# Layer 2 of a two-layer transformer kernel from one table of steps, and three weight tiles loaded earlier

## The reference

```python
x = ln(x + softmax_attention(x))          # layer 1: 16 heads of 8, rope
x = ln(x + moe16(x))                      # 16 SwiGLU experts, grouped top 4, and a shared one
# layer 2
q, k, v = x @ Wq + bq, x @ Wk + bk, x @ Wv + bv
qf, kf = elu(q @ R) + 1, elu(k @ R) + 1   # 32 features a head
kv, ks = sum_s kf * v, sum_s kf
x = ln(x + (qf @ kv / max(qf @ ks, 1e-6)) @ Wo + bo)
g = top2(softmax(x @ Rt)); g = g / (sum(g) + 1e-6)     # 8 gates a token
x = ln(x + x @ W + b + (g * (x @ A)) @ B)
```

## Time and profile before

| | us |
|---|---|
| median of three runs | 527.77 |
| lowest and highest | 526.52, 531.72 |
| profiled execution, its own time | 527.63 |
| its span in the trace | 525.8 |
| TensorE busy | 481.0, 91% of the span |
| VectorE busy | 386.0, 73% |
| ScalarE, GpSimd busy | 224.6, 106.5 |
| mean granted TensorE clock | 0.952 of full speed |

### The profile page before, as it was taken

The page is one execution under the profiler, slowest core; times in us unless marked ns, Lnnn a source line. Parts: engine busy times, 40 slices in busy tenths (PEclk is TensorE's granted clock), DMA queues, the critical chain, the costliest instruction groups (busy, mean ns, idle before and its releaser), DMA issues. The chain is left out here.

```text
span 525.8 us, 7943 instructions
## 1 busy us (share of the span) xinstructions
PE 481.0 (91%) x2903; PEld 232.8 (44%) x2903; DVE 386.0 (73%) x994; ACT 224.6 (43%) x302; POOL 106.5 (20%) x101
## 2 busy tenths in 40 slices
PE   8889899999999999989979979999999999988772
PEld 3333233334333343333335545556557456545471
DVE  6398888887898888798629796974678466655553
ACT  2306657667766656656841222231332232233110
POOL 9880427006440010000100002000011001212020
PEclk9999999999999999999999999998999799879756
DMA  4854342224322333200132113112111000000000
GB/s 155 259 142 156 90 123 92 91 70 112 115 91 70 93 86 113 66 1 22 23 80 82 60 42 100 42 60 60 41 42 51 30 20 1 21 1 0 22 20 20
DMA packets 24878, 36.31 MB, mean 69 GB/s; under 512 B 2684, under 2 KB 16258, under 8 KB 24834
## 3 DMA queue, kind: packets, MB, share of 16 engines
q1 hardware_dynamic: 24840, 35.81, 23.3%
HBM read 24.07 MB, written 11.53 MB: 68 GB/s over the span
## 5 line engine op out<-in xcount | busy, mean ns | idle before, releaser
L1092 DVE TENSOR_REDUCE negmax<-psum 128x1 f32<-128x512 f32 x256 | 169.6, 687 | 34.0 <-PE psum L521 33.8
L805 ACT ACTIVATE probs<-psum 128x1024 f32<-128x1024 f32 x128 | 127.7, 1022 | 60.1 <-PE psum L537 57.7
L521 PE MATMUL psum<-KS,QS 125*128 125x512 bf16 x256 | 98.5, 385 | 7.4 <-DVE negmax L1092 4.1
L556 PE MATMUL psum<-probs,VA 128*32 128x256 f32 x1024 | 80.5, 390 | 0.4 <-ACT probs L805 0.4
L537 PE MATMUL psum<-QS,KS 128*128 128x512 bf16 x256 | 76.0, 380 | 0.1
L784 PE MATMUL psum<-xT,late 128*128 128x512 f32 x144 | 73.3, 634 | 0.0
L521 PEld LDWEIGHTS psum<-KS,QS 125*128 125x128 bf16 x256 | 24.5, 96 | 82.0 <-DVE negmax L1092 39.9
L448 POOL TENSOR_SCALAR var<-mv 128x4 f32<-128x4 f32 x16 | 4.3, 270 | 262.6 <-DVE mv L992 262.5
L915 ACT ACTIVATE QS<-psum 128x512 f32<-128x512 f32 x36 | 21.5, 597 | 65.2 <-PE psum L784 65.2
L771 PE MATMUL psum<-late,QS 128*128 128x128 f32 x288 | 40.6, 285 | 5.7 <-DVE QS L956 3.0
L1254 DVE SCALAR_TENSOR_TENSOR QS<-QS,psum 128x512 f32<-128x512 f32 x36 | 24.5, 680 | 26.1 <-ACT QS L915 26.1
(11 more groups left out here) (148 smaller groups left out, 590.0 us busy)
## 6 DMA issues: line engine op xcount, KB each, us to landing
stack_dram<-parts SPq DMA_DIRECT2D x24, 384.0 KB, 3.3
cw<-w_dram SPq DMA_DIRECT2D x32, 256.0 KB, 3.3
KS<-stack_dram SPq DMA_DIRECT2D x16, 288.0 KB
QS<-stack_dram SPq DMA_DIRECT2D x16, 288.0 KB
late<-in_late SPq DMA_DIRECT2D x8, 346.5 KB, 4.4
res<-in_x SPq DMA_DIRECT2D x4, 256.0 KB, 3.3
w_dram<-wT SPq DMA_DIRECT2D x4, 256.0 KB, 4.4
out_y<-KS SPq DMA_DIRECT2D x4, 256.0 KB, 2.2
```

What stands on the lines that cost most here:

```text
L521: mm(sm_bank(u)[:, :], QS[b % 2][0:KROW, h, qt * P:(qt + 1) * P], KS[b % 2][0:KROW, h, :], start=True, stop=True).then_inc(sm_full, 1)
L556: last_ = mm(ps[6][32 * j:32 * j + 32, q], VA[b % 2][:, kt, h, :], probs[:, n % 2, j, q], start=(kt == 0 and half == 0), stop=(kt == NT - ...
L805: fn(probs[:, n % 2, 2 * hf:2 * hf + 2, :], psum[:, 2 * hf:2 * hf + 2, :], ACT.Exp, scale=float(DH) ** -0.5).then_inc(exp_done, 1)
L1092: V.tensor_reduce(out=negmax[:, G % 4, i:i + 1], in_=sm_bank(u)[:, :], axis=X, op=ALU.max, negate=True).then_inc(sm_free, 1)
```

## The change

One table `steps` holds every step of layer 2 for one batch with its distance in pairs from pair 9(n+1). The loop places the table for each batch, newer batch first, so that of the steps that meet in one pair those of the newer batch come first. What falls behind pair 35 is `layer2`, in the order of that table, with no pairs between. `AT` to `norm3` of the last two batches come further apart from each other in that order, or in another order than before. Only steps beside pairs are `crowded` now. And SP issues the loads of the first three `cw` tiles right after the store of batch 0's weights, before it waits for those of batch 1.

```diff
-        beside = [[] for _ in range(NB * PAIRS + 12)]
+        beside = [[] for _ in range(NB * PAIRS + 25)]
...
-        a_round = (("K", 0, 0), ("AT", 1, 0), ("K", 0, 1), ("Y1", 1, 0), ("K", 0, 2), ("ghT", 2, 0), ("K", 0, 3),
-                   ("V", 0, 0), ("norm2", 1, 0), ("Y2", 2, 0), ("Q", 0, 0), ("Q", 0, 1), ("x3T", 1, 0), ("Q", 0, 2),
-                   ("norm3", 2, 0), ("lg", 1, 0), ("Q", 0, 3), ("KV", 0, 0), ("O", 0, 1), ("O", 0, 0), ("OT", 0, 1),
-                   ("OT", 0, 0))
-        round_at = (4, 4, 5, 5, 5, 6, 6, 7, 7, 7, 8, 8, 9, 9, 9, 10, 10, 11, 12, 12, 12, 12)
-        for n in range(NB):
-            w = PAIRS * (n + 1)
-            for at, kind in ((0, "chunk"), (1, "norm1"), (3, "x2T")):
-                beside[w + at].append((kind, n, 0))
-            if n + 1 < NB:
-                for (kind, back, c), at in zip(a_round, round_at):
-                    if n >= back:
-                        beside[w + at].append((kind, n - back, c))
+        steps = ((0, "chunk", 0), (1, "norm1", 0), (4, "x2T", 0), (5, "K", 0), (5, "K", 1), (6, "K", 2), (6, "K", 3),
+                 (7, "V", 0), (7, "Q", 0), (8, "Q", 1), (8, "Q", 2), (9, "Q", 3), (9, "KV", 0),
+                 (10, "O", 1), (10, "O", 0), (11, "OT", 1), (11, "OT", 0), (12, "AT", 0), (14, "Y1", 0), (15, "norm2", 0),
+                 (17, "x3T", 0), (18, "lg", 0), (21, "ghT", 0), (22, "Y2", 0), (23, "norm3", 0))
+        for n in reversed(range(NB)):
+            for at, kind, c in steps:
+                beside[PAIRS * (n + 1) + at].append((kind, n, c))
         layer2 = [s for one in beside[NB * PAIRS:] for s in one]
         del beside[NB * PAIRS:]
-        crowded = {s for one in beside for s in one} | set(layer2)
-        for n in range(last, NB + 2):
-            layer2 += [(kind, n - back, c) for kind, back, c in a_round if 0 <= n - back < NB]
+        crowded = {s for one in beside for s in one}
...
                     if kind == "combine":
                         store_weights(a)
-            for j in range(NB * EP):
+                        if a == 0:
+                            for j in range(CW):
+                                load_weights(j)
+            for j in range(CW, NB * EP):
```

## The result

The changed kernel took 536.59 us (median of 4 runs, 532.85 to 537.10) against 527.14 us of the kernel before, also a median of 4: 1.7% slower, ratio 1.017 with a 95% interval of 1.012 to 1.022. Its profiled execution has a span of 534.5 us (before: 525.8), 8.7 us more; I had summed 2.8. Lines of the changed kernel are numbered 6 lower from TensorE's part on (L784 is L778, L700 is L694).

A forecast was written before the change was run, and what follows sets the result against it. TensorE, busy 91% of the span, was taken as the bound, so time could come only from its pauses, low-clock work or their placement. Terms -2.7 -0.3 -2.8 +0.6 +4.3 -1.8 +6.5 -1.0 = +2.8 gave 530.4 us, range 523 to 536.

The forecast's parts named there:

- slower by over 1%: Outcome above 533.1 us, given 27%: the clock rival's 22%, half of the third and a little of the main case.
- Early loads: Pair 0: issuing the first `cw` loads sooner removes TensorE's wait before `down`, -2.7 us, bounds 0 and -3.3.
- The first `x2T`: Moved from pair 12 to 13 behind `down`: its 1.21 us wait goes, a quarter counted, -0.3 us.
- `OT` in a pair of its own: Beside the pairs, `x2T` of batch 2 loses its 1.24 us wait and the low clock behind it, -2.8 us.
- `ghT` of batch 1 ahead of `x2T`: Behind the pairs, late gates delay `x2T` and the first K of batch 3, +4.3 us, bounds +2.5 and +6.
- `x3T` of batch 2: Behind the pairs, `norm2` now precedes V, so its 1.76 us wait goes, -1.8 us.
- `ghT` and `Y2` of batch 2 ahead of `Y1`: Behind `AT` of batch 3, late gates delay `Y1` and `x3T` of batch 3, +6.5 us, bounds +4.5 and +7.
- `norm3` off the last gates: Batch 2's normalisation no longer precedes batch 3's gates, which start sooner, -1.0 us, bounds 0 and -1.4.
- `lg` behind `KV`: `lg` shares `KV`'s bank and waits for its read-out; a new 0.58 us wait beside pair 27, +0.6 us.
- The low clock lasts through `O`: Rival, 22%: behind `KV`, `O` of batches 2 and 3 and pair 28's matmuls stay slow, 4.6 us more, 535.0 us.
- the two losses of the order: Behind the pairs, `ghT` of batch 1 ahead of `x2T`, +4.3 us, and `ghT` and `Y2` of batch 2 ahead of `Y1`, +6.5.

The follow-up runs named there:

- both experiments: Early loads alone added to the kernel before, 523.22 us, ratio 0.992; the same loads taken out of the changed kernel, 542.03 us, ratio 1.031.
- Putting either order back: Changed kernel with the order of before restored only behind `AT` of batch 3, 539.54 us, or only behind `OT` of batch 2, 538.88 us.
- the good order: Changed kernel with `lg` ahead of `KV` and the orders of before behind `OT` of batch 2 and `AT` of batch 3, 523.75 us, ratio 0.993.
- the kernel with `lg` ahead and one order: Changed kernel with `lg` ahead of `KV` and the order of before only behind `AT` of batch 3, 526.79 us, ratio 1.000.

## Why the prediction was wrong

The side was right (slower; forecast 0.5%), the size was not: 1.7%, just outside the range, and the 27% for slower by over 1% came true. Term by term:

- Early loads, -2.7: the wait went, 2.74 us, and both experiments give that or more (4.4 and 5.4 in medians). Right. My reading that the clock doesn't fall behind that pause was true of one execution only: without the early loads it fell in another.
- The first `x2T`, -0.3, and `OT` in a pair of its own, -2.8: both waits are gone. But 0.58 and 0.36 us came at `AT` of batch 1 and `ghT` of batch 0, for which I had claimed cover. With `lg` ahead of `KV` they are 0.28 and none.
- `ghT` of batch 1 ahead of `x2T`, +4.3: K started 10.7 us behind `AT` where I had 11.1. Right, and so is the cause (late gates).
- `x3T` of batch 2, -1.8: the wait went, but 0.89 us came at the Q step before it, which has two banks and nothing between any more. Half right.
- `ghT` and `Y2` of batch 2 ahead of `Y1`, +6.5: `x3T` 17.1 us behind `AT`, forecast 17.0. `norm3` off the last gates, -1.0: from `x3T` to the end 19.0 in place of 20.5 us, of which 0.5 is clock at the last `Y2` (1.55 in place of 2.08). Right.
- **`lg` behind `KV`, +0.6: this is the step that failed.** Its wait came, 0.67 us in three places. Its clock didn't: I let `lg` and `lh` take the low-clock stretch that `O` had and the clock be back at `O`, at no cost. But `lg` and `lh` were slow, 1.8 us over their full-clock length at each of batches 2 and 3, and `O` after them took 3.02 and 3.64 us, nearly what it had before (3.54 twice). With `KV` of batch 3, 4.83 in place of 3.76, that is 4.2 us more behind these two `KV` than before. The 1.1 of `KV` fell before `lg` began, and `KV` of batch 2 took 4.88 in the kernel with `lg` ahead, so I can't put that part down to `lg`.

In waits and clock: the sum held +4.9 of waits and -2.1 of clock (1.6 of it at `x2T` of batch 2); the trace has +5.7 and +3.0. The waits, worked out from VectorE's order link by link, were right within a microsecond in sum. The clock was wrong by 5.1: the 4.2 behind `KV`, and 1.7 at pair 10 (3.58 in place of 1.88, which the last section finds in half of all profiles), less 0.8 in several small places.

The rival *The low clock lasts through `O`*, at 22%, had the mechanism, and its 535.0 us lies close to the 536.3 of the profiled execution. That it lies so close is partly luck. It priced `O` at +1.5 twice, which came as 1.1 and 1.7 over the full clock. It also added 1.6 for the pair behind `KV` of batch 1: that pair took 3.62, but had taken 3.07 before, with `down` slow as well. My sentence that I count a low-clock stretch only where one was seen missed those rows. And pair 10 is in neither price.

The waits of the two losses of the order came as forecast, but I had taken the two losses for independent of where `lg` stands. Putting either order back gave nothing, moving `lg` gave 7.7 us, more of it from the clock than from the waits, and the orders were seen to pay only then.

## What to carry to other kernels

When a chain of short links is issued from the gaps of other steps, what counts of its position is how many gaps lie between its start and its user, not how many steps: moving its start ahead of two steps with gaps shortened the waits before its user from 3.95 and 3.42 us to 2.69 and 0.78, which reordering the users did not (4.15 and 4.01). Before calling such a wait the cause of a loss, compare TensorE's busy times: most of what this move gained was clock. Where steps follow one another with nothing dense beside them, price the matmuls at both clocks, and don't take the clock of one recorded execution for a property of the order. Dense matmuls of zeros in waits that are there anyway were worth 1.6% in the changed order; the good order without them was worth 2.4%, and both, with one more step moved, 4.3%.

## What I had not expected of the hardware

The wait of 2.6 us before `down` of pair 9 is in every profile, with the same matmuls ahead of it for over 300 us. Behind it `gate_e` and `up_e` took 1.88 us in seven of the fourteen profiles (this is the kernel with both orders and `lg` ahead) and 3.3 to 3.6 us in the other seven (as at 311.23 above):

```profile
310.40 1.13 PE L770 MATMUL psum<-late,QS 128*128 128x128 f32 x8 [2.61 <-DVE z L955]
311.37 1.88 PE L783 MATMUL psum<-xT,late 128*128 128x512 f32 x4
```

So whether a pause costs a stretch at the lower clock is not settled by the pause alone. The Trainium skill, page "TensorE: Matmul & The Clock Gate", section "HAM oscillation — how this bites in real kernels", has idle waits turn the clock down, in a kernel whose waits are longer than this one of 2.6 us; behind this shorter one the clock was down in half of the executions here. The pause of 2.74 us in pair 0, for which the prediction drew 1.6 us from that section, is shorter than the waits there too.

The clock also fell while TensorE was busy without a break, in the middle of `KV` with its matmuls of 33 columns. The kernel with `lg` ahead, batch 2:

```profile
445.00:447.00 2.00, 2.00 (x13) 2.00 (x12) 0.00 (x0) 0.00 (x0) 0.00 (x0) 0.56 0.00 0
```

Single runs of one kernel lie 1 to 2% apart (518.45 to 526.11 for the early loads alone, 522.33 to 532.63 for the kernel with `lg` ahead and one order). The mean granted clock of these runs goes the same way, 0.966 and 0.948, 0.959 and 0.929. That fits a clock that falls in some executions and not in others; why it does was not tested.
